# Output projection, layer norm and transposes between the stages of an eight-stage transformer kernel: one stream by token tiles in place of one block after another

## The reference, cut to what matters

```python
def _layernorm(x, g): return (x - mean(x)) * rsqrt(var(x) + 1e-5) * g     # over 256 channels
# x: (2, 1024, 256) float32
x = x + attn0(moe0(x))                     # 16 heads of 16, causal; Wo (256, 256)
h = cond2(x, fside, mask_k)                # below, with layernorm before and after
x = x + ffn0(h)                            # act_quant and weight_quant, conv of 3 taps, silu
x = x + attn1(cond1(x))                    # cond1 like cond2, l2-normed q and k; attn1: one head of 128
x = x + moe1(cond2(x, fside, mask_k))      # 8 experts, top 2
def cond2(x, bias, mask):
    xn = layernorm(x, g_in); q = xn @ Wq; k, v = split(xn @ Wkv)   # 16 heads of 64, one k and v
    attn = softmax(causal(q k^T + bias, mask))                      # with a null key
    return layernorm((attn @ v) @ Wo, g_out)                        # Wo (1024, 256)
def act_quant(x):    s = 127 / max(abs(x), -1);  return clip(round(x * s)) / s
def weight_quant(w): s = 1 / mean(abs(w));       return clip(round(w * s), -1, 1) / s
```

## Time and profile before

| | |
|---|---|
| median of three runs | 3602.81 us (3602.0 to 3606.71) |
| the profiled execution's own time | 3605.45 us |
| its span in the trace | 3603.7 us |
| PE busy | 3129.8 us, 87% |
| DVE busy | 1975.1 us, 55% |
| ACT busy | 1515.6 us, 42% |
| mean granted clock of PE | 0.926 |

### The profile page before, as it was taken

One profiled execution on the slowest core, in us unless ns is written; L12 is line 12 of the kernel. 1 busy time (PEld: TensorE's weight loads), 2 busy tenths in 40 slices (PEclk: granted clock), 3 DMA queues, 4 the chain that ended last, 5 costly groups with the idle time before them and its releaser, 6 DMA issues. The chain is left out here.

```text
span 3603.7 us, 50405 instructions
## 1 busy us (share of the span) xinstructions
PE 3129.8 (87%) x17344; PEld 2121.6 (59%) x17346; DVE 1975.1 (55%) x4681; ACT 1515.6 (42%) x3630; POOL 290.9 (8%) x609
## 2 busy tenths in 40 slices
PE   7998999869999996646879999978699999968996
PEld 5555666544777765332237777765357777645774
DVE  3556555345767762874457777623567777432223
ACT  1110455414666660632336666603156666312332
POOL 0003000000111100000000000000011111002222
PEclk8997999979999998867979999989799999988998
DMA  1009244027444320000162222100464445331112
GB/s 37 18 13 171 26 49 49 7 72 222 145 124 154 117 76 12 24 11 19 58 177 70 78 65 82 35 12 7 146 190 130 146 129 155 118 129 33 33 34 86
DMA packets 208731, 293.71 MB, mean 82 GB/s; under 512 B 25357, under 2 KB 145421, under 8 KB 208352
## 3 DMA queue, kind: packets, MB, share of 16 engines
q1 hardware_dynamic: 204746, 280.38, 28.1%
q0 software_dynamic: 3744, 10.23, 0.9%
HBM read 222.00 MB, written 68.10 MB: 81 GB/s over the span
## 5 line engine op out<-in xcount | busy, mean ns | idle before, releaser
L1913 ACT ACTIVATE cond_p<-cond_p,cond_negm 128x128 f32<-128x128 f32 (+7 forms) x768 | 593.1, 775 | 415.6 <-DVE cond_negm L1944 414.9
L1894 PE MATMUL ps_o<-cond_pt,cond_v 128*64 128x256 f32 (+1 forms) x3840 | 479.5, 371 | 5.2 <-DVE attn_out L1980 0.5
L1872 PE MATMUL ps_s<-cond_k_high,cond_q_high 128*128 128x512 f32 (+3 forms) x1152 | 441.1, 389 | 10.5 <-DVE cond_negm L1944 8.0
L1944 DVE CUSTOM_DVE_ANT_0 cond_p<-ps_s,cond_side,cond_null_scores 128x128 f32<-128x128 f32 (+7 forms) x512 | 404.0, 811 | 30.3 <-PE ps_s L1874 24.2
L1874 PE MATMUL ps_s<-cond_k_both,cond_q_both 128*128 128x512 f32 (+3 forms) x1152 | 388.6, 350 | 0.0
L1884 PE MATMUL ps_t<-ident,cond_p 128*128 128x128 f32 x2304 | 349.4, 281 | 6.8 <-ACT cond_pt L1918 4.8
L1894 PEld LDWEIGHTS ps_o<-cond_pt,cond_v 128*64 128x64 f32 x3840 | 237.7, 136 | 168.3 <-issue 70.5
L1884 PEld LDWEIGHTS ps_t<-ident,cond_p 128*128 128x128 f32 x2304 | 250.4, 141 | 106.6 <-issue 77.7
L1114 ACT ACTIVATE attn_pt<-ps_t 128x512 f32<-128x512 f32 (+3 forms) x384 | 172.7, 490 | 251.6 <-PE ps_t L1075 197.1
L1872 PEld LDWEIGHTS ps_s<-cond_k_high,cond_q_high 128*128 128x128 f32 x1152 | 220.7, 192 | 43.6 <-DVE cond_negm L1944 20.5
L1874 PEld LDWEIGHTS ps_s<-cond_k_both,cond_q_both 128*128 128x128 f32 x1152 | 222.7, 193 | 16.5
(11 more groups left out here) (409 smaller groups left out, 4916.5 us busy)
## 6 DMA issues: line engine op xcount, KB each, us to landing
mqa_q_halves<-cond_q_cut SPq DMA_DIRECT2D x96, 512.0 KB, 6.9
cond_q_both<-mqa_q_halves SPq DMA_DIRECT2D x384, 128.0 KB, 3.3
cond_q_high<-mqa_q_halves SPq DMA_DIRECT2D x192, 128.0 KB, 3.0
cond_side<-in_fside_16xSxS SPq DMA_DIRECT2D x32, 512.0 KB, 7.1
moe_experts<-in_L_ffn_W SPq DMA_DIRECT2D x16, 1024.0 KB, 12.6
cond_side<-in_fside_16xSxS SPq DMA_DIRECT2D x32, 448.0 KB, 5.7
cond_side<-in_fside_16xSxS SPq DMA_DIRECT2D x32, 384.0 KB, 5.1
cond_side<-in_fside_16xSxS SPq DMA_DIRECT2D x32, 320.0 KB, 4.6
```

The source lines that it names most:

```text
L1872: nc.tensor.matmul(m.S[k % 2][:, lo:hi], c32(a.Q1[i][:, h, s * P:(s + 1) * P]), c32(a.K1[:, keys]), start=True, stop=False)
L1894: last = nc.tensor.matmul(sums[u % ON][h * HD:(h + 1) * HD, s0 * P:2 * P], a.V[:, b * QB + kb, :], PT[c % PT_SLOTS][:, (2 * h + s0) * P:(h ...
L1913: nc.scalar.activation(p, p, ACT.Exp, bias=negm[u % SMALL][:, r:r + 1], scale=-1.0, accum_out=rsum[u % SMALL][:, r:r + 1]).then_inc(exped, 1)
L1944: nc.vector.tensor_tensor_reduce(out=probs(u, r, 0, q + 1), in0=m.S[k % 2][:, 0:L], in1=toep_back(u, h, L) if cosine else a.side[h][:, SID ...
```

## The change

A new function, `stage_project_norm`, does a projection, the norm behind it and its transposes in one block, tile by tile. It takes the place of `stage_project_out` with `stage_norm_turn` behind the three cond stages. Behind attn0 and attn1 the projection moves into the following cond stage and is done together with that stage's input norm (`w.front`). cond1's input norm uses it without a projection. On DVE the add, the statistics and the aggregate of tile t are followed by a piece of the group before: at t%4 = 0 the reciprocal and minus mean times reciprocal, at 1 and 2 two products with g, at 3 what `more` asks for. The subtract-and-scale moves to ACT, as an activation with two pointers (bias and scale), and is written for the input norms to a separate buffer. PE transposes group 0 behind tile 9, group 1 behind tile 13 and groups 2 and 3 at the end; ACT copies them behind its activations of two groups on.

```diff
+            def turn(g):
+                pe.wait_ge(finished, 4 * per_tile * (g + 1))
+                for c in range(DC):
+                    j = DC * g + c
+                    if j >= 2:
+                        pe.wait_ge(freed, j - 1)
...
+                for t in range(NT):
+                    if t >= 4:
+                        pe.wait_ge(taken, t - 3)
+                    for c in range(n):
+                        last = nc.tensor.matmul(m.SH[t % 4][:, 0:D], proj.heads[:, c, t * P:(t + 1) * P], proj.w[:, c, :],
+                                                start=(c == 0), stop=(c == n - 1))
+                    last.then_inc(ready, 1)
+                    if more is not None:
+                        more.tensor(pe, t)
+                    if t in (9, 13):
+                        turn((t - 9) // 4)
+            for g in range(2 if proj is not None else 0, NG):
+                turn(g)
...
+            def finish(t):
+                g = t // 4 - 1
+                if t % 4 == 0:
+                    close(g)
+                elif t % 4 < 3:
+                    weigh(4 * g + 2 * (t % 4) - 2)
+                    weigh(4 * g + 2 * (t % 4) - 1)
+                elif more is not None:
+                    dve.wait_ge(normed, 4 * g + 4)
+                    more.group(dve, g)
...
+                nc.vector.bn_stats(k.bn[:, t, :], src[:, t, :]).then_inc(stats, 1)
+                dve.wait_ge(stats, t + 1)
+                nc.vector.bn_aggr(k.mv[:, t, :], k.bn[:, t, :]).then_inc(averaged, 1)
+                if t == 0:
+                    dve.wait_ge(*g_ready)
+                if t >= 4:
+                    finish(t)
...
+            for t in range(NT, NT + 4):
+                finish(t)
...
+            for g in range(NG):
+                tiles = slice(4 * g, 4 * g + 4)
+                act.wait_ge(varied, g + 1)
+                nc.scalar.activation(k.std[:, tiles], k.std[:, tiles], ACT.Sqrt).then_inc(rooted, 1)
+                act.wait_ge(shifted, g + 1)
+                for t in range(4 * g, 4 * g + 4):
+                    nc.scalar.activation(dst[:, t, :], src[:, t, :], ACT.Identity, bias=k.nmean[:, t:t + 1],
+                                         scale=k.rstd[:, t:t + 1]).then_inc(centred, 1)
+                if g >= 2:
+                    keep(g - 2)
+            keep(NG - 2)
+            keep(NG - 1)
...
+    stage_project_norm(nc, m, name + "_in", w.front, m.X, tokens_in, m.XT, g_in, (g_loaded, 16), loop_at + 4096,
+                       also=None if cosine else loads)
...
+            pe.wait_ge(loaded, n_loads[0])
...
+    def prefetch(sp, projected):
+        sp.dma_start(m.moe1_wr[:, :, :], d["L1_ffn_Wr"].rearrange("(c p) e -> p c e", p=P)).then_inc(m.moe1_wr_loaded, 16)
+        expert_loads(sp, nc, m, d, range(4, 8))
+        sp.wait_ge(projected, NT)
+        expert_loads(sp, nc, m, d, range(4))
```

358 lines of the change are left out of this document (202 added, 156 removed).

## The result

The changed kernel takes 3482.24 us (median of 4, 3474.07 to 3483.34) where the kernel before takes 3604.76 in the same comparison: a ratio of 0.9649, 95% interval 0.9623 to 0.9675. The forecast was 3470, range 3445 to 3497. The profiled execution took 3474.07 us with a span of 3472.4, 131.4 less than the profiled one of before; the medians differ by 122.5.

What follows compares the result with a forecast made beforehand. PE bounds the loops, left alone; at six places one engine works while others wait. Gains 29.6, 36, 8.5, 27.1, 14.7 and 17.0 sum to 132.9: 3605.45 becomes 3472.5, less 2.6 to the median 3469.9, written 3470; range 3445 to 3497.

Steps and rivals of the forecast that it cites:

- A: attn0 to cond2_0: 43.8 us for 73.5, with projection 29.8, two turned groups 2.1 and tail 9.5; gain 29.6.
- B: cond2_0 to ffn0, 116.3 us: ffn0's first matmul 37.3 sooner, about 4 exposed; gain 36, between 33 and 37.3.
- C: Distance stage to cond1, no projection: 11.8 gained from the load block, 1.2 and 2.1 lost; gain 8.5.
- D: cond1 to attn1: 72.6 us for 100.1, less 0.4 for attn1's first matmuls at the lower clock; gain 27.1.
- E: attn1 to cond2_1: DVE bounds, 16 tiles at 1.47; 35.3 us for 50.1; gain 14.7.
- F: cond2_1 to moe1: SP's expert loads end the block, 77.8 us for 96.7; logits give 1.9 back; gain 17.0.
- The tail: Work left behind the last projected tile's matmuls on DVE, ACT and PE: 9.5 us in A, D and F.
- B's bias load: ffn0's start: the bias lands 7.2 us after its issue and ACT's first activation waits; about 4 exposed, part won back.
- the second rival: DVE and ACT, not PE, become the bound in the stream: 3480 to 3485 us, chance 0.14.
- The early loads: Loads hide under earlier work; rival that they don't: 14 us each in A, C and E, 3510, chance 0.08.
- Half clock in the projections: Rival: breaks between tiles hold PE at 1.2 GHz, A 27 us more, B, D and F 55 each; 3662, chance 0.03.
- The clock that stays up: Rival: shorter tails leave PE at full clock, 3 us at each of five places; 3455, chance 0.12.

Runs made afterwards that it cites:

- e2: Changed kernel with ACT's copies one group earlier, only the last group's behind all: median 3467.70 us, ratio 0.9613 to the kernel before.
- e5: Changed kernel with added matmuls that nobody reads, between the last projected tile and the last groups' transposes: 3479.47 us in one execution.
- e4: Changed kernel with the subtract-and-scale of the six norms moved back from ACT to DVE: 3481.34 us in one execution.
- e3: Changed kernel with ffn0's rounding and the transposes taken out of cond2_0's stream into a block behind it: 3500.12 us in one execution.
- e6: Changed kernel with the cond stages' loads back in a block of their own, with a wait for the last landing: 3515.51 us in one execution.
- e7: Changed kernel with w_out of the three cond stages loaded at the head of the projection's block again: 3503.03 us in one execution.
- e1: The changed kernel once more, no edit: median 3480.94 us (3471.60 to 3487.73), ratio 0.9646 to the kernel before.
- e8: Changed kernel with cond1's small loads issued in the distance stage's second block, not at the end of the first: 3478.64 us in one execution.

## Why the prediction was right, and where it was not

The kind of change was read rightly, from the brackets behind the earlier trace rows: at each of six places one engine worked while the others waited, and the floor was the projection. The measured 124 against the forecast of 132.9 comes from the terms below. They are 9 of the 12 us by which 3482.24 lies above 3470; 2 more are the kernel before, whose median was 3604.76 in this comparison and not 3602.81, and the rest is within the spread.

| place | forecast | measured | of which |
|---|---|---|---|
| A | 29.6 | 28.1 | 36.1 to the last tile for 34.0, with a stall of 2.4 that I had at nothing; 9.2 behind it for 9.8 |
| B | 36 | 32.6 | 64.6 for 62.0, with a stall of 2.7; 16.4 for 17.0; 2.7 lost behind the first matmul for 1.3 |
| C | 8.5 | 8.7 | 12.3 and -3.7 |
| D | 27.1 | 25.6 | 27.0, and 1.4 behind it for 0.4, which attn1's spread (68.1 to 71.1) can hold |
| E | 14.7 | 11.7 | 28.0 to the last tile for 26.8, with the stall of 6.5; 10.2 behind it for 8.5 |
| F | 17.0 | 17.3 | 19.0, and -1.7 for -1.9 |

**The tail** was right in size: 9.2 in A from the end of the last tile (747.2) to cond_wkv, for 9.5 and a barrier of 0.3; 16.5 in B, for 17.0; PE's wait ahead of the last two groups is 4.7 in A, D and F, for the near 4 of the prediction. Four of ACT's activations with two pointers take 2.08, or 0.52 each, the value that I took between 0.42 and 0.70; the start of one lies 0.49 behind that of the one ahead. By the figures of the Trainium skill (ScalarE: Activation LUTs, What ACT_TABLE_LOAD costs) my estimate for one back to back was 0.49; the trace agrees.

**The step that failed** is a sentence of the common part, that the transposes of groups 0 and 1 find their tokens ready "so PE adds 1.04 each for them and nothing else". The tokens were ready, the banks were not. I had followed the wait on the tokens and not the second one, on `freed`, for the second pair, although for the tail I had used that very wait. PE stood for 2.4 in A, 2.7 in B, 0.7 in D and F and 6.5 in E, 13 in all; in e2 the waits for banks behind tile 13 are gone. That the sum still came out within 9 has a part of luck: in E, where half of the 13 lies, DVE took some 1.34 a tile and not the 1.47 of the sum, and only 1.2 too much was left at the last tile. With the order of e2, in which the banks come free as the sentence assumed, and the tail is shorter besides, the median is 3467.70 for the 3470 of the forecast.

**B's bias load** was wrong as a mechanism and about right as a number. I had priced a landing of 7.2 from the earlier trace rows, which was the landing behind 2 MB of other loads; with only the 12 KB of taps ahead of it, it is 2.0. The sign that I had given for it, ACT released by a DMA, did not come. The 2.7 that B lost behind its first matmul are PE's clock (e5), against 4 charged for the bias and 1.3 after what I took to be won back. The clock was in my sum for D and F only. So B's number is close by luck.

**DVE in A** was priced at 1.7 a tile and is 1.4, so the second rival (DVE bound) was further away than I thought, and e4 came out on the other side of my expectation. In B DVE did hide, as worked out: 34.00 of 34.

**C** came out by two errors that cancel: the distance stage lost 3.7 to the loads that were put into it, not 1.2 (1.9 for the issues and 1.7 for a slower landing of its own loads, which I had not counted), and the norm, for which I had charged 2.1, lost nothing that shows.

**The early loads** were priced well, at 14 each: 15.7 in A, 11.5 in C and 13.6 in E when they are put back. For w_out I had the wait right, 6 at each place; putting it back costs 7.3 to 8.8 each, since the null row then runs at the lower clock as well.

**The overlap of the norm** is what is left, some 62 of the 124 if the parts add. Of this e3 shows the rounding's 13 to 15. No run undoes the rest by itself; for it speak the waits of 26.26 in A and their like, which are gone from the timeline, but its size is a difference.

**Half clock in the projections** did not come: 0.2165 an instruction as before and PEclk 1.00. The Trainium skill (TensorE: Matmul & The Clock Gate, A second HAM failure mode: psum-queue depth-cycling) describes, for bf16 matmuls of 512 columns, a clock that swings when PE idles briefly between groups. B does not test this: DVE kept ahead, and PE had no such breaks in the window (34.00 busy of 34). In E, where PE has 0.4 a tile and DVE 1.4, PE does wait between tiles, and the window shows 0.64, but PE is idle for half of it, as before, and these runs don't tell the one from the other.

**The clock that stays up** came true by chance only. In the first profile cond_wkv ran at 7.05 in A and E; in the second one of the same kernel it took 9.37 and 9.40. ffn0 and moe1 began at the lower clock in both (9.86 and 9.34, 8.51 and 9.53), and attn1's first sixteen took 15.18 and 14.11 for 13.78 before.

## What to carry to other kernels

Where a stage's end is projection, then norm, then transposes, each on its own engine behind a barrier, put them in one stream by tiles and issue the next stage's loads inside it: here that is worth 124 of 520 us, and the three parts (loads 38, w_out 24, overlap the rest) can each be priced from a bracket in the timeline. For every wait in the new stream ask not only whether its data are ready but also who frees its buffer and what stands ahead of that in the freeing engine's list. A load's landing time read from a trace holds for its neighbours in the queue; moved elsewhere it is another number, and it slows those it is put beside.

## What the runs showed of the hardware that I had not expected

- The same 4 KB load landed 7.2 us after its issue behind 2 MB of others and 2.0 with only 12 KB ahead of it.
- Of eight loads of 1 MB that SP issues in a row, the fifth and the seventh issue took 4.3 and 4.6 us (4.5 and 6.0 in the kernel before), each until 1.4 to 2.2 us behind the landing of the first and the third.
- A float32 matmul of 128 columns took 0.226 us at the full clock, a transpose of the same size 0.13 (1.04 for eight).
- Behind B's tail of 16.4 us with 3.9 of PE's work, ffn0's first 16 matmuls took 9.86 and 9.34 in two profiles of the same kernel; behind a tail filled with matmuls they took 7.10. Behind A's tail of 9.2 to 9.5 us with 3.5 to 3.8 of work the next stage began at either level: 7.05 in the first profile, e6 and e7, 9.35 to 9.42 in e1, e3 and e8. A first profile that shows the full clock there is no proof that it stays.
- The attention loops of the three cond stages, whose work on PE, DVE and ACT no edit changed, wander by 5 to 11 us between executions, more than most of the edits here are worth.
